# The end of an expert stage: output rows written early and completed by accumulating transfers

## The reference

```
scores = softmax(x @ gate_w.T); topk_w, topk_idx = top_k(scores, 2)        # 8 experts, 2 for each token
moe    = sum over the token's two experts of  weight * (silu(g) * u) @ w2e
shared = (silu(h @ sw1.T) * (h @ sw2.T)) @ sw3.T
x      = x + gb * (moe + shared)
```

## Time and profile before

| | us |
|---|---|
| median of 3 runs | 1146.86 (1146.69 to 1147.84) |
| the profiled execution's own time | 1147.24 |
| its span, first to last instruction | 1145.5 |
| PE busy | 1055.6 (92%) |
| DVE busy | 896.3 (78%) |
| ACT busy | 734.0 (64%) |
| POOL busy | 334.2 (29%) |
| mean granted PE clock | 0.968 |

### The profile page before, as it was taken

How to read it: one execution, slowest core, us unless ns; L and a number is a source line. 1 busy time by engine, 2 the same in 40 slices (tenths; PEclk the granted TensorE clock), 3 DMA queues, 4 the chain that set the end, 5 groups by cost and what they waited for, 6 DMA issues and landing times. The chain is left out here.

```text
span 1145.5 us, 22304 instructions
## 1 busy us (share of the span) xinstructions
PE 1055.6 (92%) x7524; PEld 919.3 (80%) x7524; DVE 896.3 (78%) x1816; ACT 734.0 (64%) x1398; POOL 334.2 (29%) x335
## 2 busy tenths in 40 slices
PE   5988888869999999999999999999999997979994
PEld 4756666658899899899899898898898986769992
DVE  5798988856788788788788788788788787857765
ACT  4679797766766666666666666666666763615650
POOL 3353544442311201211211111111111244753440
PEclk9799999989999999999999999999999998989997
DMA  7210001010401311321311311221221292834426
GB/s 255 94 52 16 15 6 56 2 50 23 135 20 52 112 46 47 106 46 51 101 50 52 98 53 53 97 54 53 86 65 54 91 37 100 329 99 120 124 89 225
DMA packets 70264, 92.13 MB, mean 80 GB/s; under 512 B 22609, under 2 KB 50385, under 8 KB 69170
## 3 DMA queue, kind: packets, MB, share of 16 engines
q1 hardware_dynamic: 66786, 81.83, 25.7%
q0 software_dynamic: 3408, 9.39, 2.2%
HBM read 46.35 MB, written 42.75 MB: 78 GB/s over the span
## 5 line engine op out<-in xcount | busy, mean ns | idle before, releaser
L1551 PE MATMUL all_psum<-all_h_parts,attn_wp 128*128 128x512 f32 x1140 | 296.2, 395 | 0.0
L1551 PEld LDWEIGHTS all_psum<-all_h_parts,attn_wp 128*128 128x128 f32 x1140 | 209.1, 188 | 39.5
L1723 ACT CAST attn_pp<-attn_p 128x512 fp32r<-128x512 f32 (+3 forms) x256 | 117.4, 459 | 188.4 <-DVE attn_p L1831 186.2
L1812 DVE TENSOR_TENSOR attn_pp<-attn_p,attn_pp 128x512 fp32r<-128x512 f32 (+3 forms) x256 | 198.0, 773 | 6.5 <-ACT attn_pp L1723 6.5
L1970 POOL TENSOR_TENSOR all_gate<-all_gate,attn_sq 128x512 f32<-128x512 f32 x64 | 84.7, 1324 | 368.6 <-ACT attn_sq L1734 368.5
L1630 PE MATMUL all_psum<-attn_qkp 128*128 128x512 f32 (+3 forms) x768 | 164.6, 323 | 3.7 <-DVE attn_qkp L1812 3.7
L1577 PE MATMUL all_psum<-attn_pp,attn_vp 128*128 128x512 f32 (+3 forms) x768 | 163.3, 321 | 1.1 <-DVE attn_pp L1812 0.5
L1577 PEld LDWEIGHTS all_psum<-attn_pp,attn_vp 128*128 128x128 f32 x768 | 128.9, 189 | 21.6 <-issue 1.5
L1630 PEld LDWEIGHTS all_psum<-attn_qkp 128*128 128x128 f32 x768 | 124.1, 189 | 12.4 <-issue 4.3
L1831 DVE TENSOR_TENSOR attn_p<-all_psum,attn_mask 128x512 f32<-128x512 f32 (+3 forms) x256 | 123.4, 482 | 3.6 <-PE all_psum L1630 2.5
L1054 DVE TENSOR_REDUCE front_top<-all_psum 128x2 f32<-128x256 f32 (+3 forms) x128 | 99.3, 814 | 16.4 <-PE all_psum L695 15.1
(11 more groups left out here) (375 smaller groups left out, 1892.9 us busy)
## 6 DMA issues: line engine op xcount, KB each, us to landing
expert_rows<-attn_empty SPq DMA_DIRECT2D x8, 2080.0 KB, 13.6
expert_weight_parts<-all_wraw SPq DMA_DIRECT2D x32, 304.0 KB, 2.4
experts_wx<-expert_weight_parts SPq DMA_DIRECT2D x8, 1216.0 KB, 16.7
all_wraw<-in_w1p SPq DMA_DIRECT2D x8, 1024.0 KB, 6.0
all_yacc<-expert_rows SPq DMA_DIRECT2D x39, 130.5 KB, 2.2
all_wraw<-in_wx SPq DMA_DIRECT2D x16, 304.0 KB, 3.0
attn_mask<-decay_masks SPq DMA_DIRECT2D x16, 256.0 KB, 2.6
experts_wx<-expert_results SPq DMA_DIRECT2D x6, 512.0 KB, 8.2
```

The lines of the kernel that those rows point to most:

```text
L1551: last = nc.tensor.matmul(out, wp[:, a, k, col:col + P], hh[:, c, k, b * S:(b + 1) * S], start=(m == 0), stop=(m == 5))
L1723: nc.scalar.copy(pp[:, u % 2, 0, cols], p[:, cols]).then_inc(p_hi, 1)
L1812: nc.vector.tensor_tensor(out, whole, high.bitcast(F32), ALU.subtract).then_inc(ready, 1)
```

## The change

x is stored to the output during the loop: from tile 8 on, at every second tile, SP issues the store of one batch. The tail no longer adds to x. The gated sums are added to the output in DRAM by seven transfers with an accumulate operation, issued by POOL. The token number becomes 16 * partition + tile, so that one partition's results of consecutive tiles lie side by side: a part of two tiles is read in contiguous pieces of 2 KB, one of four tiles in 4 KB. The parts are six, in another order (0:2, 12:16, 2:4, 4:8, 8:10, 10:12), which makes twelve loads. PE now adds the results of three pairs (12:14, 14:16 and 10:12, the last into a third bank), DVE those of the rest. `gates(LATE)` stands behind the last `down_of`.

```diff
-        nc.gpsimd.iota(self.number[:, :], [[P, NT]], base=0, channel_multiplier=1, **exact).then_inc(self.number_ready, 1)
+        nc.gpsimd.iota(self.number[:, :], [[1, NT]], base=0, channel_multiplier=NT, **exact).then_inc(self.number_ready, 1)
...
-        PARTS = [slice(0, 2), slice(2, TB)] + [slice(b * TB, (b + 1) * TB) for b in range(1, B)]
+        LAST = slice((B - 1) * TB, NT)
+        PARTS = [slice(0, 2), LAST, slice(2, TB), slice(TB, 2 * TB), slice(2 * TB, 2 * TB + 2), slice(2 * TB + 2, 3 * TB)]
+        BY_TENSOR = [slice(LAST.start, LAST.start + 2), slice(LAST.start + 2, NT), PARTS[5]]
+        DONE = [PARTS[0], PARTS[2], BY_TENSOR[0], PARTS[3], BY_TENSOR[1], PARTS[4], PARTS[5]]
...
+        both = t["y_dram"][0:2 * B * S].rearrange("(c p t) n -> c p t n", c=2, t=NT)
...
+                    if j >= RING1 and j % 2 == 0 and j - RING1 < 2 * B:
+                        b = (j - RING1) // 2
+                        if b < B - 1:
+                            sp.wait_ge(x_added, b + 1)
+                        else:
+                            sp.wait_ge(norm.x_new, B - norm.FIRST)
+                        sp.dma_start(t["out"][:, rows(b), :], x[:, rows(b), :]).then_inc(x_stored, 16)
                 for r in range(RING1):
                     sp.wait_ge(y_sent[r], len(range(r, TILES, RING1)) * 16)
-                both = t["y_dram"][0:2 * B * S].rearrange("(c t p) n -> c p t n", c=2, p=P)
                 for i, part in enumerate(PARTS):
                     for c in range(2):
                         sp.dma_start(results[:, c, part, :], both[c, :, part, :]).then_inc(results_in[i], 16)
-                done = PARTS[:-1] + [slice(NT - TB, NT - 2), slice(NT - 2, NT)]
-                for i, part in enumerate(done):
-                    sp.wait_ge(x_final, i + 1)
-                    sp.dma_start(t["out"][:, part, :], x[:, part, :]).then_inc(stored, 16)
-                sp.wait_ge(stored, 16 * len(done))
+                sp.wait_ge(stored, 16 * len(DONE))
...
-                    if s == TILES + 2:
-                        gates(LATE)
                     if s >= 3:
                         down_of(s - 3, at_expert.pop(s - 3))
+                gates(LATE)
                 ups(LATE)
...
-                pe.wait_ge(results_in[B], 32)
-                for half in range(2):
+                for i, part in enumerate(BY_TENSOR):
+                    pe.wait_ge(results_in[1 if i < 2 else 5], 32)
                     for c in range(2):
-                        tt = (B - 1) * TB + 2 * half
-                        last = nc.tensor.matmul(bank(Y_BANK + half), t["ident"][:, :],
-                                                results[:, c, tt:tt + 2, :].rearrange("p t n -> p (t n)"),
-                                                start=False, stop=(c == 1))
+                        last = nc.tensor.matmul(bank(Y_BANK + i), t["ident"][:, :],
+                                                results[:, c, part, :].rearrange("p t n -> p (t n)"),
+                                                start=(i == 2 and c == 0), stop=(c == 1))
                     last.then_inc(pair_made, 1)
...
+                def by_vector(part):
+                    i, n = PARTS.index(part), DONE.index(part)
+                    y = results[:, 0, part, :]
                     dve.wait_ge(results_in[i], 32)
                     nc.vector.tensor_tensor(y, y, results[:, 1, part, :], ALU.add).then_inc(y_sum, 1)
+                    dve.wait_ge(y_sum, sum(p not in BY_TENSOR for p in DONE[:n + 1]))
+                    nc.vector.tensor_tensor(y, y, gate_rows(part), ALU.mult).then_inc(y_gated, 1)
-                    nc.vector.tensor_tensor(xb, xb, y, ALU.add).then_inc(x_final, 1)
+                def by_tensor(part):
+                    i = BY_TENSOR.index(part)
+                    y = results[:, 0, part, :]
+                    dve.wait_ge(pair_made, i + 1)
+                    nc.vector.tensor_tensor(y, ps[:, Y_BANK + i, :].rearrange("p (t n) -> p t n", t=2), gate_rows(part),
                                             ALU.mult).then_inc(y_gated, 1)
+                for part in DONE:
+                    if part in BY_TENSOR:
+                        by_tensor(part)
+                    else:
+                        by_vector(part)
...
+                pool.wait_ge(x_stored, 16 * B)
+                for i, part in enumerate(DONE):
+                    pool.wait_ge(y_gated, i + 1)
+                    nc.gpsimd.dma_start(t["out"][:, part, :], results[:, 0, part, :], accum_op=ALU.add).then_inc(stored, 16)
```

More of the change, by code:

```diff
@@ L2388, in experts_stage @@
         results_in, pair_made = n.sems("results_in", len(PARTS)), n.sem("pair_made")
-        y_sum, y_gated, x_final, stored = n.sem("y_sum"), n.sem("y_gated"), n.sem("x_final"), n.sem("stored")
+        y_sum, y_gated, x_stored, stored = n.sem("y_sum"), n.sem("y_gated"), n.sem("x_stored"), n.sem("stored")
         def bank(i):
@@ L2885, in _, with gate_rows @@
                 lower(LATE + 1)
-                for i, part in enumerate(PARTS[:4]):
+                def gate_rows(part):
+                    b = part.start // TB
+                    return t["gate"][:, 3, b:b + 1, :].to_broadcast([P, part.stop - part.start, D])
+                def by_vector(part):
+                    i, n = PARTS.index(part), DONE.index(part)
+                    y = results[:, 0, part, :]
                     dve.wait_ge(results_in[i], 32)
-                    y, xb = results[:, 0, part, :], x[:, part, :]
-                    b = part.start // TB
@@ L2890, in _ @@
                     nc.vector.tensor_tensor(y, y, results[:, 1, part, :], ALU.add).then_inc(y_sum, 1)
-                    dve.wait_ge(y_sum, i + 1)
-                    nc.vector.tensor_tensor(y, y, t["gate"][:, 3, b:b + 1, :].to_broadcast([P, part.stop - part.start, D]),
-                                            ALU.mult).then_inc(y_gated, 1)
-                    dve.wait_ge(y_gated, i + 1)
-                    nc.vector.tensor_tensor(xb, xb, y, ALU.add).then_inc(x_final, 1)
[L2896 to L2904, removed]
```

## The result

The changed kernel is slower: 1152.70 us median against 1147.77 for the kernel before beside it, ratio 1.0042 (95% interval 1.0029 to 1.0055). The forecast was 1143.8, faster. The profiled execution has a span of 1149.0; with 1150.69 us it is the fastest of the five, 2.0 under their median.

A forecast was written before the change was run, and what follows sets the result against it. The tail was taken as bound by transfers first, then PE, DVE and one store; scatter, loads, accumulates, PE/DVE and last landing summed to an end at 1142.4, 3.1 us gained: 1146.86 - 3.1 = 1143.8 us, range 1141.5 to some 1149.5.

The forecast's parts named there:

- The last scatter goes earlier: End of the scatters: with the gates moved, the last starts at 1116.34 instead of 1117.20, -0.86 us.
- The loads: Tail loads: pieces of 2 and 4 KB run faster, 10.8 us instead of 12.0, -1.1 us (bounds 0 and -1.8).
- The accumulates beside the loads: Tail: three accumulates ready before the loads end push the last part back 2.07 us (bounds 0 and 4.1).
- f = 1: Tail transfers: an accumulate costs f times a copy's time on the DMA engines; 1 was taken, 2 the upper bound.
- rival A: Tail accumulates take two reads, f = 2: load delay 4.1 us, last accumulate 0.7 longer, 1146.6 us; chance 0.28.
- PE and DVE in the tail: Behind the last landing: one pair on PE, 3.81 us, then one DVE multiplication, 0.69; DVE ends at 1139.4.
- The last accumulate: After DVE's end: 3.0 us until the last accumulate lands, where 2.4 stood before, +0.6 us.
- Rival B: DMA engines from 1121.0 to the end: the accumulating queue becomes the bound; at f = 3 1150.8 us; chance 0.17.
- Rival C: Tail: the accumulates fill gaps only, the last part lands at 1132.8, 1141.7 us; chance 0.08.
- Hidden edits: Loop stores, POOL's new wait and scatter rows 16 KB apart: taken as 0, 1 us either way for the last scatter's landing.

The follow-up runs named there:

- b4: The kernel before with only the token number as 16 * partition + tile and loads in pieces of 2 and 4 KB; ratio 1.0001 to the kernel before.
- c1: The changed kernel without accumulates and without stores in the loop; VectorE adds all seven parts to x, SyncE stores them; ratio 0.9985 to the kernel before.
- f1: The changed kernel with a GpSimd drain between its last scatter and its first accumulate; ratio 1.0019 to the kernel before.
- a2: The changed kernel with the last three of seven parts added by VectorE and stored by SyncE; ratio 0.9996 to the kernel before.
- a1: The changed kernel with its seven accumulates turned into plain copies, the addition of x left out; ratio 1.0012 to the kernel before.
- h1: The changed kernel with plain copies for accumulates (addition of x left out) and GpSimd's drain ahead of them; median 1143.83 us, ratio 0.9958 to the kernel before.
- c2: c1 with GpSimd, after an early drain, adding tiles 2:4 and 4:8 to x in place of VectorE; ratio 0.9985 to the kernel before.
- b5: The kernel before plus the four stores of x in the loop, the tail storing the finished x again; ratio 0.9989 to the kernel before.

## Why the prediction was wrong

- **The last scatter goes earlier**: right (1.26 us apart, -0.86).
- **The loads**: mis-sized. -1.1 us was taken for wider pieces; b4 shows about 0 to 0.5 and c1, with its other order, 14.6 us to the last landing against 15.1 before. The changed kernel's own loads cannot be told from what ran beside them. The price of a piece came from a stretch at a steady rate and left out the slow first microseconds.
- **The accumulates beside the loads**: the last part landed after 16.5 us with accumulates and after 14.6 without (c1), 1.9 us, close to the 2.1 taken. But the agreement is luck and no proof of f = 1. Other profiles give 17.2 and 17.3 with accumulates (f1, a2), 15.4 and 16.4 with copies (a1, h1) and 14.7 with neither (c2): copies cost 0.7 to 1.8 us and accumulates 1.8 to 2.7, where the sum had 2.1 and rival A 4.1. That at f = 2 fewer of them got in front of the loads and the rest piled up behind fits this, but was not shown.
- **PE and DVE in the tail**: right within 0.3 us (3.5 us on PE, VectorE idle for 1.9 us ahead of its last operation).
- **The last accumulate**: the step that failed. It was priced at 2.7 us from issue to landing with f = 1, and took 6.5 at f = 2.0 to 2.3. Rival A's price for one at f = 2 is 3.4, so of the 3.8 us too much some 3.1 are queueing behind the three accumulates before it, for which the sum had no term. I took 1 because mixed loads and stores ran at 396 GB/s; those are one read for each write, and an accumulate is two. That row did not bear on the question. Rival A had f right. That its end (26.3 us after the first load) lies only 1.2 us before the measured landing (27.5) is partly luck: it had the last part land after 18.0 us (measured 16.5) and the last accumulate take 3.4 (measured 6.5).
- **The drain**: in neither the sum nor a rival. I counted that the kernel ends 2.4 us after VectorE because it had ended so before, and did not ask what else had to end by then. GpSimd's drain lay in the trace, at the block's own line, hidden by 21 us of tail; giving GpSimd the last transfer brought it to the end, 3.3 us.
- Rival B named the side and the place, and its sign came: a last accumulate of more than 4 us, and DMA engines full (share 0.88 to 1.11 in every window) from 1120 to 1142. It needed an f above 2.1, which the measured 2.0 to 2.3 straddle, and priced f = 3; the drain it did not have. Neither cause alone makes the loss: without the drain the ratio is still 1.0019, with copies in place of the accumulates still 1.0012. Rival C falls.
- **Hidden edits**: right. Loop, row order in the scatters and the waits of SyncE cost nothing that shows (from the last scatter's issue to the first load's 2.54 us, before 2.53).

Put together: the tail's 31.0 us are the forecast's 23.5, plus 3.8 for the last landing, plus 3.3 for the drain, plus 0.4 of small differences.

## What to carry to other kernels

An engine that issues nothing at the end can hide a long drain; before giving it the last transfer, look at the sequencer lines of the block's end, and drain it in an idle stretch (7.6 us of drain under the loads made the last one end 0.3 us after the landing). Price an accumulating transfer as two copies or a little more on the DMA engines (2.0 to 2.3 here), add the queue in front of it, and keep it off a stretch where they are full. An addition moved from VectorE to GpSimd is not free if both read SBUF at once.

## What the runs showed of the hardware that I had not expected

- A drain of GpSimd took 5.87 us with none of its transfers in flight after 71 scatters, 0.04 us when nothing had been issued since another drain, and ended 0.3 us behind the landing with seven transfers owed. With 71 scatters and the seven accumulates owed (changed) its end came 8.9 us behind the end of GpSimd's last issue and 3.3 us behind the landing, against 5.9 us behind the last issue in the kernel before, and 0.3 us behind the landing in f1. Why it was longer than either, and whether its length goes by the number of transfers, stays open.
- The clock of PE for the pairs behind the last landing differs between executions: eight passes took 6.79 us in the kernel before but 5.33 in b5 (mean granted clock 0.54 and 0.70), four took 3.48 in the changed kernel but 1.98 in c1 and h1 (0.56 and 1.00). This alone moves a single profile's tail by 1.5 us, so b4's and b5's shorter tails say less than their ratios.
